# The first batch of a fused attention and expert kernel: other semaphore for b1's rows, latents read by two engines, another order of the first value units

## The reference

```python
x = x + tanh(g_xattn) * attention(ctx, layernorm(x))     # 16 batches, 256 latents and 256 media rows of 256
#   q = ln(x) Wq + bq;  k, v = [ln(ctx); ln(x)] Wkv + bkv;  8 heads of 128, 512 keys;  softmax;  Wo, bo
x = x + tanh(g_ffn) * experts(layernorm(x))              # top 2 of 8 experts, silu(x W1 + b1) W2 + b2
```

## Time and profile before

| | us |
|---|---|
| median of three runs | 1560.92 (1560.53 to 1563.27) |
| the profiled execution | 1558.27, of which the span is 1556.6 |
| PE busy | 1503.6 (97% of the span) |
| DVE busy | 1110.2 (71%) |
| ACT busy | 950.6 (61%) |
| POOL busy | 604.3 (39%) |

### The profile page before, as it was taken

The page is one execution under the profiler, slowest core; times in us unless marked ns, Lnnn a source line. Parts: engine busy times, 40 slices in busy tenths (PEclk is TensorE's granted clock), DMA queues, the critical chain, the costliest instruction groups (busy, mean ns, idle before and its releaser), DMA issues. The chain is left out here.

```text
span 1556.6 us, 29904 instructions
## 1 busy us (share of the span) xinstructions
PE 1503.6 (97%) x10410; PEld 1386.2 (89%) x10410; DVE 1110.2 (71%) x2687; ACT 950.6 (61%) x2060; POOL 604.3 (39%) x714
## 2 busy tenths in 40 slices
PE   6999998999999999999999999999989999999986
PEld 5889887888989889898888988888989999999986
DVE  6777776777777777777777777777786666666674
ACT  5655654565565555555565565555777777777764
POOL 5322423233342433433234342332454544444452
PEclk9999999999999999999999999999999999999998
DMA  4000100001000000000000000022754544554553
GB/s 147 19 21 8 21 8 21 8 22 28 8 22 8 22 28 8 22 8 21 12 17 29 7 22 8 8 75 70 193 128 127 154 131 127 146 139 127 147 157 69
DMA packets 57823, 91.13 MB, mean 59 GB/s; under 512 B 8521, under 2 KB 44774, under 8 KB 57550
## 3 DMA queue, kind: packets, MB, share of 16 engines
q1 hardware_dynamic: 41710, 70.19, 14.0%
q0 software_dynamic: 15824, 18.98, 6.9%
q10 hardware_dynamic: 144, 0.05, 0.0%
HBM read 70.91 MB, written 18.29 MB: 57 GB/s over the span
## 5 line engine op out<-in xcount | busy, mean ns | idle before, releaser
L876 POOL TENSOR_SCALAR probs<-probs,rsum 128x512 f32<-128x512 f32 x256 | 174.1, 692 | 531.6 <-DVE rsum L1547 523.7
L1087 ACT ACTIVATE pt_hi<-turn 128x512 fp32r<-128x512 f32 x256 | 139.3, 595 | 239.7 <-PE turn L1233 239.7
L901 POOL DMA_INDIRECT out_rows<-yo,token x71 | 121.5, 1711 | 213.5 <-DMA out_rows<-yo,token 137.6
L1664 DVE TENSOR_TENSOR ht_lo<-hs,ht_hi 128x512 fp32r<-128x512 f32 x142 | 98.0, 690 | 114.5 <-ACT ht_hi L1052 113.0
L1541 DVE TENSOR_REDUCE smax<-score 128x1 f32<-128x512 f32 x256 | 169.8, 685 | 12.8 <-PE score L183 12.4
L986 ACT ACTIVATE probs<-score,nbias 128x512 f32<-128x512 f32 x256 | 173.0, 685 | 4.2 <-DVE nbias L1543 4.1
L1043 ACT ACTIVATE hs<-ph,vecs 128x256 f32<-128x256 f32 (+1 forms) x284 | 114.2, 457 | 95.6 <-PE ph L183 82.4
L1772 DVE TENSOR_TENSOR pt_lo<-turn,pt_hi 128x512 fp32r<-128x512 f32 x256 | 164.2, 682 | 9.4 <-ACT pt_hi L1087 9.3
L181 PE MATMUL py<-w_hi,ht_lo 128*128 (+1 forms) x568 | 163.9, 289 | 5.8 <-DVE ht_lo L1664 5.8
L182 PE MATMUL py<-w_lo,ht_hi 128*128 (+1 forms) x568 | 161.8, 285 | 0.0
L183 PE MATMUL py<-w_hi,ht_hi 128*128 (+1 forms) x568 | 161.7, 285 | 0.0
(11 more groups left out here) (247 smaller groups left out, 4709.7 us busy)
## 6 DMA issues: line engine op xcount, KB each, us to landing
w_raw<-in_L_ffn_W SPq DMA_DIRECT2D x45, 1024.0 KB, 12.8
xhat_rows<-rows SPq DMA_DIRECT2D x16, 264.0 KB, 2.2
x_raw<-in_x SPq DMA_DIRECT2D x16, 256.0 KB, 3.1
c_raw<-in_ctx SPq DMA_DIRECT2D x16, 256.0 KB, 3.2
out_rows<-x SPq DMA_DIRECT2D x16, 256.0 KB, 2.3
xg<-xhat_rows,token POOLq DMA_INDIRECT x71, 4.3
out_rows<-yo,token POOLq DMA_INDIRECT x71
v_raw<-in_L_xattn_Wkv SPq DMA_DIRECT2D x2, 512.0 KB, 8.6
```

The source lines that it names most:

```text
L876: last = pool.tensor_scalar(probs[n % 2][:, t, :], probs[n % 2][:, t, :], rsum[:, n % 2, t:t + 1], 1.0, ALU.mult, ALU.mult)
L901: pool.indirect_dma_start(out=A["out"], out_offset=bass.IndirectOffsetOnAxis(ap=token[:, u:u + 1].bitcast(U32), axis=0), in_=yo[t % N_YO][ ...
L1087: act.activation(pt[0][:, 2 * t:2 * t + 2, :], turn[t][:, :].rearrange("p (j i) -> p j i", j=2), ACT.Copy).then_inc(s_pthi, 1)
```

## The change

- `vec_rows` keeps the first 32 rows; b1's 64 rows get a buffer and a semaphore of their own. PE turns the latents first, then the 32 vector rows; b1's rows are turned in step 1 ahead of scores 1, and ACT copies them behind the units of step 1. The first output projection waits for that copy, and for Wo's pieces.
- Turned latents go the way the media half went: ACT writes high parts, DVE writes `zt`, one k each at a time, into another pair of banks.
- q0 is loaded and split ahead of k0; ACT copies k0 behind the latents.
- `before` holds only the first value unit. The other three of the first half stand in step 0, behind k and q of step 1.
- ACT copies q1 and v1 at the end of step 0 (before: between the value units), and DVE splits q1 there. Wo's pieces move from the end of step 0 to the end of step 1, tanh and `constants()` from step 1 to step 2.

```diff
-    before = [("z", (0, k)) for k in range(KD)] + [("q", 0), ("k", 0)] + [("v", (0, w)) for w in range(JT)]
+    before = [("z", (0, k)) for k in range(KD)] + [("q", 0), ("k", 0), ("v", (0, 0))]
     steps = []
...
         m, w = (i - 1) // JT + 1, (i - 1) % JT
-        if i and m < 2 * B:
+        if i == 0:
+            units += [("v", (0, w)) for w in range(1, JT)]
+        elif m < 2 * B:
             units.append(("v", (m, w)))
...
         vec_rows = sb("vec_rows", [P, P])
+        b1_rows = sb("b1_rows", [P, P])
         raw.update(k1=sb("k1_raw", [P, KD, INNER - FIRST_W]), q1=sb("q1_raw", [P, KD, INNER - FIRST_W]),
...
-            return turn[0][:, k * T:(k + 1) * T] if half else score[k][:, 0:T]
+            return (turn if half else score)[k][:, 0:T]
...
         s_wlo = {"dve": sem("weights_lo_dve"), "pool": sem("weights_lo_pool")}
-        s_media0, s_zt1 = sem("kvt0_media"), sem("zt0_media")
+        s_first, s_zt1 = sem("kvt0_first"), sem("zt0_ready")
         s_ve0, s_rs0 = sem("ve0"), sem("rs0")
...
         s_w2 = [sem(f"w2_in{i}") for i in range(E)]
-        s_b2, s_home_b2 = sem("b2_in"), sem("home_b2_in")
+        s_b1, s_b2, s_home_b2 = sem("b1_in"), sem("b2_in"), sem("home_b2_in")
         N_GN = N_XG * SUB
...
         N_PAD = 2 + -(-LISTS // P)
-        N_VEC, N_SMALL = 7, 4
+        N_VEC, N_SMALL = 6, 4
...
         rest = INNER - FIRST_W
-        pieces = [columns("k0", 0, FIRST_W, "pool"), columns("q0", 0, FIRST_W, "pool"),
+        pieces = [columns("q0", 0, FIRST_W, "pool"), columns("k0", 0, FIRST_W, "pool"),
                   columns("v0", 0, HALF, "dve"), columns("k1", FIRST_W, rest, "pool"),
...
             load(0)
-            load_weights("k0", "q0", "v0", "k1", "q1", "v1")
+            load_weights("q0", "k0", "v0", "k1", "q1", "v1")
             load(1)
...
                 pool.tensor_tensor(rs_a[:, cols], ve["a"][:, cols], minus_half[:, cols], ALU.pow).then_inc(s_rs0, 1)
-            lo_weights(pool, "pool", "k0", "q0", "k1", "v1")
+            lo_weights(pool, "pool", "q0", "k0", "k1", "v1")
             for i in range(STEPS + 2):
...
                 row += n
-            act.dma_start(vec_rows[B1:VECS, :], A["L0_ffn_b1"].rearrange("e (g p) -> (e g) p", p=P)).then_inc(s_vec, 16)
+            act.dma_start(b1_rows[0:VECS - B1, :], A["L0_ffn_b1"].rearrange("e (g p) -> (e g) p", p=P)).then_inc(s_b1, 16)
...
-            def first_turned(out, half, k):
-
-                return act.activation(out[:, k, half * T:(half + 1) * T], first_bank(half, k), ACT.Identity,
+            def first_turned(half, k):
+
+                return act.activation(kvt[0][0][:, k, half * T:(half + 1) * T], first_bank(half, k), ACT.Identity,
                                       scale=gamma[:, half, k:k + 1], bias=beta[:, half, k:k + 1])
...
-            hi_weights(act, "k0", "q0")
+            hi_weights(act, "q0")
             act.wait_ge(s_vt, 1)
-            act.activation(vecs[:, :], proj[:, 0:VECS], ACT.Copy).then_inc(s_vecs, 1)
+            act.activation(vecs[:, 0:B1], proj[:, 0:B1], ACT.Copy).then_inc(s_vecs, 1)
             act.wait_ge(s_vecs, 1)
             act.wait_ge(s_zt0, 1)
-            for out in (kvt[0][0], zt):
-                for k in range(KD):
-                    last = first_turned(out, 1, k)
-            last.then_inc(s_lat0, 1)
+            first_turned(1, 0).then_inc(s_first, 1)
+            act.wait_ge(s_zt1, 1)
+            first_turned(1, 1).then_inc(s_lat0, 1)
+            hi_weights(act, "k0")
             act.wait_ge(s_full, KD)
-            first_turned(kvt[0][0], 0, 0).then_inc(s_media0, 1)
-            act.wait_ge(s_zt1, 1)
-            first_turned(kvt[0][0], 0, 1).then_inc(s_aread, KD)
+            first_turned(0, 0).then_inc(s_first, 1)
+            act.wait_ge(s_zt1, 3)
+            first_turned(0, 1).then_inc(s_aread, KD)
             hi_weights(act, "v0")
...
                 hi_part(*u)
-                for unit, name in ((("k", 0), "k1"), (("v", (0, 0)), "q1"), (("v", (0, 2)), "v1")):
-                    if u == unit:
-                        hi_weights(act, name)
+                if u == ("k", 0):
+                    hi_weights(act, "k1")
             for i in range(STEPS + 2):
...
                 if i == 0:
+                    hi_weights(act, "q1", "v1")
+                if i == 1:
+                    act.wait_ge(s_vt, 2)
+                    act.activation(vecs[:, B1:VECS], proj[:, 0:VECS - B1], ACT.Copy).then_inc(s_vecs, 1)
                     hi_weights(act, "o0", "o1")
-                if i == 1:
+                if i == 2:
                     act.wait_ge(s_small, 16 * N_SMALL)
...
                 b, h = n // H, n % H
+                if n == 0:
+                    pe.wait_ge(s_vecs, 2)
+                    weights_split(pe, "o0")
+                    weights_split(pe, "o1")
                 wait_read(pe, ("o", n))
...
             pe.wait_ge(s_ident, 1)
-            pe.wait_ge(s_vec, 16 * N_VEC)
-            pe.transpose(proj[:, 0:VECS], vec_rows[0:VECS, :], ident[0:VECS, 0:VECS]).then_inc(s_vt, 1)
             pe.wait_ge(s_z0, 1)
             turn_first(TT).then_inc(s_zt0, 1)
+            pe.wait_ge(s_vec, 16 * N_VEC)
+            pe.transpose(proj[:, 0:B1], vec_rows[0:B1, :], ident[0:B1, 0:B1]).then_inc(s_vt, 1)
             pe.wait_ge(s_z, 1)
...
             for i in range(STEPS + 2):
-                if i == 2:
-
-                    weights_split(pe, "o0")
-                    weights_split(pe, "o1")
+                if i == 1:
+                    pe.wait_ge(s_b1, 16)
+                    pe.wait_ge(s_vecs, 1)
+                    pe.transpose(proj[:, 0:VECS - B1], b1_rows[0:VECS - B1, :], ident[0:VECS - B1, 0:VECS - B1])\
+                        .then_inc(s_vt, 1)
                 if i < STEPS:
...
             first_rows(TT, c_raw[0]).then_inc(s_z, 1)
-            dve.wait_ge(s_lat0, 1)
-            dve.tensor_tensor(kvt[0][1][:, :, T:KEYS], zt[:, :, T:KEYS], kvt[0][0][:, :, T:KEYS].bitcast(F32),
-                              ALU.subtract).then_inc(s_kvl0, 1)
             dve.wait_ge(s_vecs, 1)
-            dve.wait_ge(s_full, KD)
-            for k in (1, 0):
-                if k == 0:
-                    dve.wait_ge(s_media0, 1)
-                dve.tensor_scalar(zt[:, k, 0:T], first_bank(0, k), gamma[:, 0, k:k + 1], beta[:, 0, k:k + 1],
-                                  ALU.mult, ALU.add).then_inc(s_zt1, 1)
-            dve.wait_ge(s_zt1, 2)
-            dve.wait_ge(s_aread, KD)
-            dve.tensor_tensor(kvt[0][1][:, :, 0:T], zt[:, :, 0:T], kvt[0][0][:, :, 0:T].bitcast(F32), ALU.subtract)\
-                .then_inc(s_kvt, 1)
+            for half, cols, full, hi_ready, done in ((1, slice(T, KEYS), (s_zt0, 1), (s_lat0, 1), s_kvl0),
+                                                     (0, slice(0, T), (s_full, KD), (s_aread, KD), s_kvt)):
+                dve.wait_ge(*full)
+                for k in (1, 0):
+                    if k == 0:
+                        dve.wait_ge(s_first, 2 - half)
+                    dve.tensor_scalar(zt[:, k, cols], first_bank(half, k), gamma[:, half, k:k + 1],
+                                      beta[:, half, k:k + 1], ALU.mult, ALU.add).then_inc(s_zt1, 1)
+                dve.wait_ge(s_zt1, KD * (2 - half))
+                dve.wait_ge(*hi_ready)
+                dve.tensor_tensor(kvt[0][1][:, :, cols], zt[:, :, cols], kvt[0][0][:, :, cols].bitcast(F32), ALU.subtract)\
+                    .then_inc(done, 1)
             lo_weights(dve, "dve", "v0")
...
                 read_unit(*u)
-                if u == ("v", (0, 1)):
-                    lo_weights(dve, "dve", "q1")
+
             def constants():
...
                     prepare_a(1)
+                    lo_weights(dve, "dve", "q1")
+                if i == 1:
                     lo_weights(dve, "dve", "o0", "o1")
-                if i == 1:
+                if i == 2:
                     constants()
...
                     prepare_a(b + 2, h - A_STEP + 1)
```

## The result

The changed kernel takes 1564.5 us (median of 18 runs) where the kernel before takes 1559.7 (median of 18 on the same chip): a ratio of 1.0031, interval 1.0024 to 1.0038, or 4.8 us slower. One of the 18 took 2109.76 us at a mean granted clock of 0.654 and is left out of the ratio. The profiled execution of the changed kernel took 1564.52, with a span of 1562.8, against 1558.27 and 1556.6 before: 6.2 more.

The account below looks back on a forecast made before the run. The prediction took the matmul engine, busy 1503.6 of 1556.6 us, as the bound. Its terms, 0.85 + 1.1 + 2.1 + 1.6 = 5.65 us, on 1558.27 plus the median's 2.65 surplus, gave 1566.6, range 1561 to 1570.5.

Parts of the forecast that it names:

- T3: Start of PE's turn of probabilities 3; the forecast's terms, up to the stall in step 3, sum to 5.65 us.
- T0: Start of PE's turn of probabilities 0: forecast at 33.05 us, 0.85 later than before.
- parts 1 to 3: Start, new order and wait for probabilities 0: start's 2.5 us gain all spent, their turn 0.85 later.
- part 4: PE's clock behind the turn of probabilities 0: 4 us at half speed, +1.1 us, between 0 and 2.5.
- part 5: Wo moved behind step 1: its splits delay DVE's maximum of step 2, PE stalls 2.1 us, between 0 and 2.5.
- part 6: Constants moved to step 2: the maximum of step 3 ends 2.5 late, PE stalls 1.6 us, between 0 and 2.5.
- part 2: New order up to the third value unit: new wait of 0.45 at scores 0, last value unit ending at 24.5.
- the later stalls are absorbed: Rival, steps 2 and 3: only parts 3 and 4 count, +1.95 us, giving 1562.9; chance 0.22.
- more is lost: Rival: vectors land with b1 (+1.1) and clock stays low for the whole stretch (+1.4), giving 1569.1; chance 0.15.
- the start's gain is kept: Rival at the start: something lets POOL scale probabilities 0 near 29.5, giving 1558; chance 0.03.
- The rival of the pause: ACT's unexplained pause at 235 us goes with memory placement: 7 us less, 1559.6 or 1556.9; chance 0.08.
- T1: Start of PE's turn of probabilities 1: forecast at 42.25 us, 1.95 later than before.

Follow-up runs that it names:

- e5: Changed kernel with POOL's split of v1 behind its scaling of probabilities 0 instead of ahead of it; ratio to before 0.9999.
- e8: Changed kernel with DVE's split of q1 moved behind its low parts of probabilities 0 in step 1; one execution timed, 1564.11 us.
- e2: Changed kernel with both halves of Wo's split back at the end of step 0; ratio to before 1.0034.
- e4: Changed kernel with 48 unused turns of the identity on PE behind scores 1, while it waits for probabilities 0; ratio to before 1.0031.
- e9: Kernel before with 27 unused turns of the identity on PE ahead of scores 1; ratio to before 0.9943.
- e3: Changed kernel with tanh and the constants back in step 1, behind Wo; ratio to before 1.0035.
- e6: e1 with 27 unused turns of the identity on PE ahead of scores 1; ratio to before 0.9925.
- e10: Changed kernel with 27 unused turns of the identity on PE behind scores 1; ratio to before 0.9990.
- e1: Kernel before with the new start alone: q0 first, b1's rows apart, latents read by two engines; ratio to before 0.9978.
- e7: Changed kernel with the start of the kernel before, so the new order alone; ratio to before 1.0044.
- e11: e1 with 13 unused turns of the identity on PE ahead of scores 1; ratio to before 0.9915.
- e12: e1 with 27 unused turns of the identity as PE's first work; ratio to before 0.9933.

## Why the prediction was right

The sign and the chain of waits held, and the cost, 5.33 us at T3, was forecast as 5.65. That the sum is this close is partly luck, since two of its terms miss by half a us in opposite directions. By the terms of the sum:

| term | forecast | measured |
|---|---|---|
| T0 (parts 1 to 3) | +0.85 | +1.40 |
| clock (part 4) | +1.1 | +0.57 |
| step 2, Wo (part 5) | +2.1 | +1.79 |
| step 3, constants (part 6) | +1.6 | +1.57 |
| T3 | +5.65 | +5.33 |

*Parts 1 to 3.* The first queries were forecast for 10.8 and came at 10.72; the vectors had landed by 7.84. The miss lies in part 2: the last value unit began at 23.67 instead of 23.1. Of that, 0.3 was there at scores 0, which began at 17.10 instead of 16.8: the first keys took 2.70 us of PE (12.63 to 15.33), where they had taken 2.24 before, since 128x512 matmuls ran at 0.63 us until 16.2 and at 0.40 behind that. PE, slower by this, came just as the keys' split ended, so the forecast wait of 0.45 doesn't show as one. Another 0.23 is a wait for the queries of step 1. DVE's bias of probabilities 0, at 20.07, took 1.17 us for two elements per partition, while POOL's k1 split ran from 17.71 to 21.22; ACT's exponentials waited 0.44 for it, and the queries were copied and split later. The forecast had priced DVE against POOL where both split weights, and for the bias in step 3, but not here. The last value unit also ended 1.67 behind its start, not 1.4, so ACT's copies were done at 28.29 instead of 27.6. The rest followed as forecast: POOL's v1 2.34 (2.25 forecast), then the scaling, 2.86 with DVE's q1 split beside it, together 5.3 to T0 (5.45 forecast). e5 and e8 take this apart: the place of v1 in POOL's queue is worth 6.7 us of T0, and the q1 split beside the scaling 1.8.

That a DVE instruction with two inputs in SBUF and a POOL instruction that reads SBUF shut each other out was the Trainium skill's rule (SBUF — State Buffer, "Who interferes with whom"), and the 4.86 us of e2 and the 1.36 of e8 agree with it. The row of the bias fits the page's other sentence, that `tensor_scalar` can take both ports: it ended at 21.24, when POOL's split ended (21.22). No run took this apart.

*Part 4.* The low clock was forecast as 4 us behind T0 and lasted 3.0 (33.61 to 36.6). The 4 us were a misreading: they counted from 29.95, where PE began again, but the window 30.0 to 30.5 was still granted 1.00. e4 puts the price of the 3.0 at 1.4, where the forecast had 2.0 (four us at half speed). The stretch of before, 8.08, is 0.8 above e4's 7.27, so the term is 0.57, half of the 1.1. This is the term most wrongly sized, and it balances the miss of T0. Nor was the 0.9 of before the price of the clock, as the forecast had it: e9 has the full clock and the longer stretch. It was DVE's queue with Wo in it, which the change took out of this stretch.

*Parts 5 and 6.* e2 and e3 undo one each, and the stall of its step goes, by 1.78 and by 1.57. The rival that the later stalls are absorbed falls with these two. That more is lost had two conditions, and neither came: the vectors had landed by 7.84, not with b1, and the low clock ended well inside the stretch, at 36.6. That the start's gain is kept would have needed the scaling of probabilities 0 near 29.5; it began at 30.69, behind v1, as forecast.

*The whole time.* The forecast of 1566.6 against 1564.5 measured is 1.2 of starting point (1560.92 was the median of three runs of before, and 18 gave 1559.69) and 0.8 of cost. As a bare time 1564.5 even lies nearer to the 1562.9 of the absorbed stalls than to 1566.6; it is the difference to before (4.8, against 5.65 and 1.95) and e2 and e3 that tell the two apart. The difference of medians, 4.8, is a little below T3's 5.33; the interval (3.7 to 5.9) holds it.

*The rival of the pause* did not happen: the pause stayed, at the same place. But e6, e9 and e10 show that it was a real possibility, and a cheap one: another count of matmuls far ahead of it takes some 8 us away.

e1's gain and the change's loss are therefore both explained: the start gives 2.6 at T0 (2.3 at T3), the later copies and splits of v1 and q1 take it and 1.4 more before T0, and the moved Wo splits and constants each cost more than the slack of the step that they are moved to.

## What to carry to other kernels

Before work is moved "to where there is room", look at the in-order queues of the engines that do it: here each piece was small, but on POOL it stood ahead of the one operation that PE waited for, and on DVE ahead of the maxima. The old order had one stall, of 3.4 us; the new one has three, of 6.5, 1.5 and 1.3. Before a low clock is priced, ask whether the engine would have had to wait anyway: in the kernel before it cost nothing at T1, since DVE's queue was as long. Try the parts of such a change alone; the start was worth 2.3 us and was hidden by the rest. When the profile shows a stand of several us that nothing explains, time a version with a few harmless instructions more before reading a ratio below 1% as the effect of an edit.

## What the runs showed of the hardware

**A pause that comes and goes with the number of PE's instructions.** By one profiled execution of each, before, after, e1, e2, e3, e5, e7 and e8 all have it at step 25, 6.7 to 9.6 us long, though T3 lies anywhere from 54.67 (e1) to 66.35 (e7). e6, e9, e10, e11 and e12, with 13 or 27 matmuls more, don't; e4, with 48 more, has three others elsewhere. Smaller ones of 1.1 to 1.6 us, at steps 17, 18 and 33, are in e9, e11 and e12, and one in e2. In the changed kernel PE had finished the output unit that the pausing ACT operation reads at about 240.6, and ACT began it at 246.11. In e10 ACT began the same one at 240.64:

```profile
240.64 0.47 ACT L981 ACTIVATE ot_hi<-ring,vecs 128x256 fp32r<-128x256 f32 x1 [0.66 <-PE ring L185]
```

ACT's own instructions are the same in both. So ACT, not the data that the trace names, was late. Since the pause keeps its step while T3 moves by 11.7 us, it is not tied to a moment of the run either. Whether it is the fetch of instructions, whose place in memory the extra ones shift, was not tried. The Trainium skill (Runtime: NRT & Kernel Launch, "Instruction fetch mechanics") calls the cost of such fetches mostly hidden; no run here shows that they are the cause.

**A DVE operation of two elements per partition that takes 1.17 us,** beside POOL's reading of two tensors, where the same bias took 0.17 in the next step (33.56 to 33.73). Its end is POOL's end within 0.03 us: 21.24 and 21.22 here, 20.86 and 20.84 in e4 (where it took 0.78), 30.46 and 30.43 in e8 (0.96), and 50.49 and 50.47 before. Not every POOL operation does this: in e5 the bias at 33.54 took 0.17 inside a POOL power operation of 128x4 (32.72 to 33.75).

**The clock.** In the kernel before, PE stood for 3.38 us until 29.95, was still granted 1.00 when it began again, and was granted 0.50 from about 30.5 to 33.9. In the changed kernel the clock fell at about 29.8, within the stand of 6.5 us, and stayed low for 3.0 us behind T0; in e7 5.5. In e10 the 27 turns filled the stand's first 3 us only: the clock fell at about 32.9, still before T0, and T0–T1 was 8.59, no better. In e6 27 turns filled the stand, in e11 13 filled half of it, and the clock stayed at 1.00 in both; T1 was not sooner, since DVE's keys' split came 1.27 and 1.28 behind PE. At the start the granted figure misleads: it reads 1.00 in the changed kernel from 12 to 16 us, while a 128x512 matmul takes 0.63 us, as it does at 0.50 behind T0, and 0.40 from 16.2 on.
